# The softmax denominator's broadcast matmul in bf16 instead of f32, in a fused attention and MoE kernel

## The chip, the cores and the metric

The kernel runs on one Trainium2 chip as one program on all 8 cores. The metric is the device time of a run in microseconds, that of the slowest core. A core has TensorE (PE, matmuls into PSUM), VectorE (DVE), ScalarE (ACT, activation functions), GpSimd (POOL, which here only issues DMAs) and SyncE (SP, likewise).

## What is computed

The input x has 4 sequences of 4096 tokens with 1024 features. The layer is attention with 16 heads whose queries and keys are 6-vectors, followed by a mixture of 8 experts, each with a residual and a layer norm:

```python
x_bigram = concatenate([x, x_prev], -1)
L_q = exterior(x_bigram @ W1_q, x_bigram @ W2_q)   # per head, 6 values, normalized
L_k = exterior(x @ W1_k, x @ W2_k)
attn = einsum('bqhc,bkhc->bhqk', L_q, L_k @ _J6.T) * 6.0 ** (-0.5)
attn = softmax(where(causal, attn, -inf))
out = einsum('bhqk,bkhd->bqhd', attn, x @ W_v + b_v) @ W_o + b_o
x = layernorm(x + out)
# MoE: router softmax, top 2 of 8 experts, h = silu(x @ w_gate) * (x @ w_up), h @ w_down
x = layernorm(x + moe(x))
```

## The kernel before

Each core takes one sequence's keys and values (two cores share a sequence) and half of its query tiles: 16 tiles of 128 rows. The program has three blocks, one behind the other.

- The first block transposes x, projects values, keys and queries, and leaves `Vs` (values of 32 key tiles, per head 64 columns and a 65th of ones), `JLKT` (keys) and `LQT` (queries) in SBUF.
- The second block is attention with the output projection, the first layer norm and the router. It is the one that the change touches.
- The third block is the MoE, expert by expert, with weights loaded from HBM, and the last layer norm.

In the second block the query tiles are taken in four groups of four (`g`, 512 query columns at once). Group g needs K = 8g + 8 key chunks of 128. Heads are taken in eight pairs (a, b). For each key chunk `kc` (a step):

1. `emit_score` (L444): PE computes the scores of a and of b (L457, keys by queries, 128 by up to 512 into one of three PSUM banks `pS`), and ACT takes exp(scale * score) into `PT`, bf16 (L467). For the last 8 chunks DVE multiplies 128 columns by the causal mask (L474).
2. `emit_av` (L480): PE accumulates `Vs[kc, h]` (65 columns) by `PT` into `pAV0` or `pAV1`, 65 partitions by 512 (L488). The 65th row, from the column of ones, is the sum of the exponentials, that is the softmax denominator. There is one bank for even heads and one for odd heads, so the next pair's first accumulation waits until the last pair's has been read.

The division is a chain for each head, in three functions. `emit_chain_pre` (L504): DVE copies row 64 of `pAV` to `srow` on one partition (L509), then PE spreads it over 64 partitions by a matmul of a row of 64 ones with `srow` (L519) into `pWO[0:64, 512:1024]`. `emit_chain_act` (L523): ACT takes Ln of it (L525) and Exp of minus that (L528), which gives 1/sum in `rbr`. `emit_chain_post` (L533): DVE multiplies `pAV[0:64]` with `rbr` into `attnT`, bf16 (L536), and so frees the bank.

The order is written out by hand in the loop over pairs (L547). Within step kc the scores of kc are issued ahead of the AV matmuls of kc - 1. The last pair's chains are put into the next pair's first steps: `pre` and `act` of head a and then of head b behind the scores of step 0, `post` of both behind the scores of step 1. On PE the two L519 of a border so stand between the scores of step 0 and those of step 1, and on ACT the Ln and Exp of both heads stand between the exponentials of step 0 and step 1. All chains use the same `srow` and the same PSUM columns: the copy of b waits for the matmul of a (semaphore `rbm`), and the matmul of b waits for the Exp of a (semaphore `rbr`). Behind the last pair of a group the chains run alone: that of head 14 twice (L570, L571), then that of head 15. Then follow, for each of the four tiles, the output projection (L585), the residual, the layer norm and the router.

Of the kernel before, what the change touches and what calls it, by code (L numbers as in the profile page):

```python
# [8 lines left out]
F32 = mybir.dt.float32  # L9
BF16 = mybir.dt.bfloat16  # L10
# [59 lines left out]
def build_program(debug=0, phases=3):  # L70
# [45 lines left out]
    with ExitStack() as _st0:  # L116
# [11 lines left out]
        with ExitStack() as _st1:  # L128
# [4 lines left out]
            with ExitStack() as _stA:  # L133
# [30 lines left out]
                P = Prog()  # L164
# [184 lines left out]
                if debug >= 3:  # L349
                    JL_D3 = P.val("jl")  # L350
                    P.emit("gpsimd", lambda g: g.dma_start(out=dbg["kk"], in_=kk_sb[:]),
                           waits=[("jl", JL_D3)], inc="dbgs", inc_n=16)
# [4 lines left out]
                if debug >= 1:  # L357
                    JL_D = P.val("jl")
                    P.emit("gpsimd", lambda g: g.dma_start(out=dbg["vs"], in_=Vs[:]),
                           waits=[("jl", JL_D)], inc="dbgs", inc_n=16)  # L360
# [9 lines left out]
                       waits=[("wA", W_SETUP), ("dbgs", P.val("dbgs"))])  # L370
# [8 lines left out]
            with ExitStack() as _stB:  # L379
                sbB = lambda *a: _stB.enter_context(nc.sbuf_tensor(*a))  # L380
# [7 lines left out]
                
                wo_sb = sbB("wo_sb", [128, 8, 1024], BF16)
                bob = sbB("bob", [128, D], F32)  # L390
                srow_t = sbB("srow", [1, 512], F32)
                ones1 = sbB("ones1", [1, 64], F32)
                
                rbl_t = sbB("rbl", [64, 512], F32)
                rbr0 = sbB("rbr0", [64, 512], F32)
# [27 lines left out]
                P = Prog(cnt1)  # L423
                PT = [PT0, PT1, PT2, PT3]
                pS, pAV = [pS0, pS1, pS2], [pAV0, pAV1]
                pWO = pWO0
# [4 lines left out]
                    out=wo_sb[:], in_=wo_h.rearrange("(dc p) n -> p dc n", p=128)), inc="wB", inc_n=16)  # L431
                P.emit("gpsimd", lambda g: g.dma_start(out=bob[:], in_=bob_h), inc="wB", inc_n=16)
                W_B = P.val("wB")
                P.emit("vector", lambda v: v.memset(ones1[:], 1.0), waits=[("bar1", 5)])
                P.emit("vector", lambda v: v.drain(), inc="xt")
                ONES_RDY = P.val("xt")

# [56 lines left out]
                for g in range(NG):  # L494
# [4 lines left out]
                        waits=[("bar1", 5), ("msk", P.cnt.get("_mskuse_%d" % (g - 1), 0))],  # L499
# [4 lines left out]
                    def emit_chain_pre(hh):  # L504
                        hbb = hh % 2
                        srw = [("av", av_counts[hh])]
                        if rbm_vals:
                            srw.append(("rbm", max(rbm_vals.values())))
                        P.emit("vector", lambda v, hbb=hbb: v.tensor_copy(  # L509
                            srow_t[0:1, :], pAV[hbb][64:65, :]), waits=srw)  # L510
                        P.emit("vector", lambda v: v.drain(), inc="sr")  # L511
                        sr_vals[hh] = P.val("sr")
                        rw = [("sr", sr_vals[hh]), ("xt", ONES_RDY)]
                        prev_rbr = rbr_vals[hh - 1] if (hh - 1) in rbr_vals else last_rbr
                        if prev_rbr:
                            rw.append(("rbr", prev_rbr))
                        rw.append(("y1a", P.val("y1a")))
                        def rbmm(te):
                            return te.matmul(pWO[0:64, 512:1024], ones1[:], srow_t[0:1, :], start=True, stop=True)  # L519
                        P.emit("tensor", rbmm, waits=rw, inc="rbm")  # L520
                        rbm_vals[hh] = P.val("rbm")

# [19 lines left out]
                    def emit_chain(hh):  # L542
                        emit_chain_pre(hh)
                        emit_chain_act(hh)
                        emit_chain_post(hh)

                    for p in range(8):  # L547
                        a, b = 2 * p, 2 * p + 1
                        prev_a = prev_b = None
                        for kc in range(K):  # L550
                            sinfo_a = emit_score(g, a, kc)
                            sinfo_b = emit_score(g, b, kc)
                            if p >= 1:
                                if kc == 0:
                                    emit_chain_pre(2 * p - 2)
                                    emit_chain_act(2 * p - 2)
                                    emit_chain_pre(2 * p - 1)
                                    emit_chain_act(2 * p - 1)
                                elif kc == 1:
                                    emit_chain_post(2 * p - 2)  # L560
                                    emit_chain_post(2 * p - 1)
                            if kc >= 1:
                                emit_av(g, a, kc - 1, prev_a)
                                emit_av(g, b, kc - 1, prev_b)
                            prev_a, prev_b = sinfo_a, sinfo_b
                        emit_av(g, a, K - 1, prev_a)
                        emit_av(g, b, K - 1, prev_b)
                        av_counts[a] = P.val("av") - 1
                        av_counts[b] = P.val("av")
# [5 lines left out]
                    for qq in range(4):  # L575
# [4 lines left out]
                            waits=[("bar1", 5), ("y1a", P.val("y1a"))], inc="xqd", inc_n=16)  # L580
                        def womm(te, qq=qq):
                            ins = None
                            for cp in range(8):
# [11 lines left out]
                               waits=[("wo", WO_T), ("xqd", P.val("xqd"))])  # L595
# [14 lines left out]
                               waits=[("v1", P.val("v1"))])  # L610
# [4 lines left out]
                               waits=[("sd1", P.val("sd1"))])  # L615
# [6 lines left out]
                        def tph(te, qt=qt):  # L622
                            ins = None
                            for dc in range(8):
# [4 lines left out]
                               waits=[("tpf", P.val("tpf"))])  # L629
                        P.emit("vector", lambda v: v.drain(), inc="xft")  # L630
                        def tpl(te):
                            ins = None
                            for dc in range(8):
# [4 lines left out]
                               waits=[("tpf", P.val("tpf"))])  # L638
# [5 lines left out]
                        def rtmm(te, qb=qb):  # L644
# [3 lines left out]
                            for src, w in srcs:  # L648
# [8 lines left out]
                            waits=[("rt", P.val("rt"))])  # L657
# [3 lines left out]
                            waits=[("rmax", P.val("rmax"))])  # L661
# [3 lines left out]
                               waits=[("rexp", P.val("rexp"))])  # L665
# [27 lines left out]
                if debug >= 2:  # L693
                    P.emit("gpsimd", lambda g: g.dma_start(out=dbg["acc"], in_=acc_t[:]),
                           waits=[("xf", P.val("xf"))], inc="dbgs", inc_n=16)
                    P.emit("gpsimd", lambda g: g.dma_start(out=dbg["comb"], in_=comb_t[:]),
                           waits=[("cmb", P.val("cmb"))], inc="dbgs", inc_n=16)
                    P.emit("gpsimd", lambda g: g.dma_start(out=dbg["attnT"], in_=attnT[:]),
                           waits=[("ate", P.val("ate"))], inc="dbgs", inc_n=16)
# [6 lines left out]
                       waits=[("wB", W_B), ("dbgs", P.val("dbgs"))])  # L706
# [8 lines left out]
        with ExitStack() as _stD:  # L715
# [23 lines left out]
            P = Prog(cnt2)  # L739
# [5 lines left out]
            for t in range(NSLOT):  # L745
                def tpx(te, t=t):
                    ins = None
                    for dc in range(8):
# [4 lines left out]
                       waits=[("bar2", 5), ("tpf", P.val("tpf"))])  # L753
# [3 lines left out]
            for e in range(NE):  # L757
                P.emit("gpsimd", lambda g, e=e: g.dma_start(  # L758
                    out=wg_sb[:], in_=wg_h[e].rearrange("(dc p) (hc q) -> p hc dc q", p=128, q=128)),
                    waits=[("bar2", 5), ("gmm", 44 * e)], inc="wg", inc_n=16)  # L760
                P.emit("gpsimd", lambda g, e=e: g.dma_start(
                    out=wu_sb[:], in_=wu_h[e].rearrange("(dc p) (hc q) -> p hc dc q", p=128, q=128)),
                    waits=[("bar2", 5), ("umm", 44 * e)], inc="wu", inc_n=16)
                P.emit("gpsimd", lambda g, e=e: g.dma_start(
                    out=wd_sb[:], in_=wd_h[e].rearrange("(hc p) n -> p hc n", p=128)),
                    waits=[("bar2", 5), ("dmm", 16 * e)], inc="wd", inc_n=16)

            for e in range(NE):
                for tc in range(4):
                    for hc in range(NHC):  # L770
                        gi = (tc * NHC + hc) % 2
                        def gmm(te, hc=hc, tc=tc, gi=gi, e=e):
                            ins = None
                            for dc in range(8):
# [5 lines left out]
                               waits=[("wg", 16 * (e + 1)), ("xft", XFT_ALL),  # L780
                                      ("sg", P.val("sg") - 1)], inc="gmm")
                        def umm(te, hc=hc, tc=tc, gi=gi, e=e):
                            ins = None
                            for dc in range(8):
# [5 lines left out]
                               waits=[("wu", 16 * (e + 1)), ("hm", P.val("hm") - 1)], inc="umm")  # L790
                        P.emit("scalar", lambda s, gi=gi: s.activation(sG[gi][:], pG[gi][:], AF.Silu),  # L791
                               waits=[("gmm", P.val("gmm")), ("hm", P.val("hm") - 1)])
# [3 lines left out]
                            waits=[("sg", P.val("sg")), ("umm", P.val("umm"))])  # L796
                        P.emit("vector", lambda v: v.drain(), inc="hm")
                HM_E = P.val("hm")
                for t in range(NSLOT):
                    def dmm(te, t=t):  # L800
                        ins = None
                        for hc in range(NHC):
# [7 lines left out]
                           waits=[("wd", 16 * (e + 1)), ("hm", HM_E), ("acc", P.val("acc"))],  # L810
                           inc="dmm")
                    if e == NE - 1:
# [3 lines left out]
                            waits=[("dmm", P.val("dmm"))])  # L816
                    else:
# [3 lines left out]
                            waits=[("dmm", P.val("dmm"))])  # L821
                    P.emit("vector", lambda v: v.drain(), inc="acc")  # L822
                    if e == NE - 1:
                        ob = t % 2
                        P.emit("vector", lambda v: v.tensor_scalar(st2[:, 0:1], st2[:, 0:1], 1.0 / D, None, ALU.mult),
                               waits=[("acc", P.val("acc"))])
# [8 lines left out]
                               waits=[("ln2", P.val("ln2"))])  # L835
# [5 lines left out]
                            waits=[("sd2", P.val("sd2")), ("out", 16 * t)])  # L841
# [3 lines left out]
                            waits=[("eo", P.val("eo"))], inc="out", inc_n=16)  # L845
# [71 lines left out]
```

How the kernel before makes its waits and increments, by code:

```python
    def replay(self, eng_name, handle, sems):  # L51
        for fn, waits, inc, inc_n in self.ops[eng_name]:
            for s, v in waits:
                handle.wait_ge(sems[s], v)
            ins = fn(handle)
            if inc is not None:
                if ins is None:
                    raise RuntimeError(f"op with inc {inc} returned no instruction")
                ins.then_inc(sems[inc], inc_n)
```

## Time and profile before

| what | value |
|---|---|
| times of two runs | 4463.73 and 4864.91 us |
| their median | 4664.32 us |
| the profiled execution, its own time | 4461.65 us |
| its span on the slowest core (core 4) | 4458.6 us |
| spans of the 8 cores | 4441.5 to 4458.6 us |
| mean granted TensorE clock of the 8 cores | 0.768 to 0.770 |
| busy: PE, weight loads, DVE, ACT, POOL | 3320.7, 1306.4, 1192.7, 952.0, 95.1 us |

The span goes from a core's first instruction to its last; the time of a run is 3 us more in the profiled execution. Busy times are sums over the whole span and say nothing on which engine a stage waits for. The granted clock is the share of the full 2.4 GHz that TensorE gets; 0.50 is the lower of its two levels, 1.2 GHz. The profile also has groups of instructions by line, the sums of who waited for whom, and the instructions in order of time, in which a bracket behind an instruction gives how long its engine was idle before it and what ended that. In a name such as `pS` the number of the buffer is left out.

### The profile page before, as it was taken

How to read it: one execution, taken by the hardware profiler on the slowest of the kernel's cores; microseconds unless marked ns; L12 is line 12 of the kernel's file. 1: busy time of each engine (PE TensorE's matmuls, PEld its weight loads, DVE VectorE, ACT ScalarE, POOL GpSimd, SP SyncE). 2: the span in 40 equal slices, each digit the busy share in tenths (PEclk: the TensorE clock that was granted, in tenths of full speed). 3: DMA queues.
4: the chain of work that ended last, by engine and by line, in shares of the span. 5: the costliest groups of instructions: out<-in, count | busy, mean ns of one | idle time of the engine just before them, and what ended most of it. 6: DMA issues, size and time to landing. Idle time of an engine off the chain costs nothing. (4 is left out here: it accounts for less than half of the span.)

```text
span 4458.5 us, 49278 instructions; the slowest of 8 cores (4441.5 to 4458.6 us)
## 1 busy us (share of the span) xinstructions
PE 3320.7 (74%) x14263; PEld 1306.4 (29%) x14476; DVE 1192.7 (27%) x3454; ACT 952.0 (21%) x1948; POOL 95.1 (2%) x42
## 2 busy tenths in 40 slices
PE   3444432556866896799945979898898979899896
PEld 1222222112112111111113434343343434344342
DVE  3444454233123113211142121121212112121126
ACT  0000000323533563466610101010010101011010
POOL 0000000000000000000000000000000000000000
PEclk8777655555555555555556999999999999999999
DMA  3111122000000000000007060515114051513301
GB/s 69 34 34 34 42 77 62 17 8 15 1 8 14 1 1 12 10 1 1 1 15 78 1 65 14 52 27 52 27 19 60 1 52 27 52 27 30 49 1 76
DMA packets 215020, 129.85 MB, mean 29 GB/s; under 512 B 188640, under 2 KB 188640, under 8 KB 214768
## 3 DMA queue, kind: packets, MB, share of 16 engines
q0 software_dynamic: 200944, 76.35, 14.7%
q1 hardware_dynamic: 13824, 50.34, 3.5%
q8 instruction: 134, 2.20, 0.2%
q14 instruction: 118, 0.97, 0.1%
HBM read 192.51 MB, written 8.39 MB: 45 GB/s over the span
## 5 line engine op out<-in xcount | busy, mean ns | idle before, releaser
L804 PE MATMUL pD<-wd_sb,ht 128*128 128x512 bf16 x2760 | 624.7, 379 | 200.6 <-DVEq L822 189.4
L488 PE MATMUL pAV<-PT,Vs 128*65 128x512 bf16 (+3 forms) x1280 | 624.4, 563 | 105.3 <-DVEq L539 55.0
L467 ACT ACTIVATE PT<-pS 128x512 bf16<-128x512 f32 (+3 forms) x1280 | 613.0, 531 | 384.7 <-PE pS L457 372.6
L785 PE MATMUL pU<-xfT,wu_sb 128*128 128x512 bf16 x2760 | 661.7, 380 | 25.6 <-DMA wu_sb<-w_up 22.6
L775 PE MATMUL pG<-xfT,wg_sb 128*128 128x512 bf16 x2759 | 661.9, 380 | 4.3 <-DVEq L754 1.4
L791 ACT ACTIVATE sG<-pG 128x512 bf16<-128x512 f32 x352 | 210.1, 597 | 1748.1 <-PE pG L775 1748.1
L794 DVE TENSOR_TENSOR ht<-sG,pU 128x512 bf16<-128x512 bf16 x352 | 241.8, 687 | 997.5 <-PE pU L785 997.5
L804 PEld LDWEIGHTS pD<-wd_sb,ht 128*128 128x128 bf16 x2816 | 266.2, 97 | 559.1 <-issue 256.5
L785 PEld LDWEIGHTS pU<-xfT,wu_sb 128*128 128x128 bf16 x2816 | 275.8, 98 | 356.5 <-issue 25.2
L775 PEld LDWEIGHTS pG<-xfT,wg_sb 128*128 128x128 bf16 x2816 | 276.0, 98 | 335.0 <-issue 4.3
L457 PE MATMUL pS<-LQT,JLKT 6*128 6x512 bf16 (+3 forms) x1280 | 358.0, 537 | 4.4 <-ACT PT L467 2.2
L474 DVE TENSOR_TENSOR PT<-PT,masks_g 128x128 bf16<-128x128 bf16 x512 | 115.4, 225 | 831.9 <-ACT PT L467 777.1
L818 DVE SCALAR_TENSOR_TENSOR acc<-pD,comb,acc 128x1024 bf16<-128x1024 f32 x112 | 143.7, 1283 | 582.1 <-PE pD L804 582.1
L488 PEld LDWEIGHTS pAV<-PT,Vs 128*65 128x65 bf16 x1280 | 140.4, 140 | 402.0 <-issue 395.8
L287 PE MATMUL pTk<-ident,Lsc 128*6 128x128 bf16 x768 | 28.7, 301 | 304.2 <-DVEq L279 304.2
L519 PE MATMUL pWO<-srow,ones 1*64 1x512 f32 x136 | 131.5, 1068 | 108.7 <-DVEq L511 61.6
L457 PEld LDWEIGHTS pS<-LQT,JLKT 6*128 6x128 bf16 x1280 | 71.6, 99 | 430.8 <-issue 425.2
L302 PE MATMUL pV<-wvks,xT 128*128 128x512 bf16 (+1 forms) x740 | 183.3, 416 | 3.9 <-issue 3.1
L214 PE MATMUL pT<-ident,xab 128*128 128x128 bf16 x512 | 64.7, 306 | 127.2 <-DVEq L210 127.2
L258 ACT ACTIVATE rln<-ssb 128x16 f32<-128x16 f32 x48 | 10.3, 215 | 689.0 <-DVEq L257 689.0
L625 PE MATMUL pT<-ident,acc 128*128 128x128 bf16 x128 | 16.2, 306 | 145.1 <-DVEq L620 145.1
L302 PEld LDWEIGHTS pV<-wvks,xT 128*128 128x128 bf16 x768 | 84.6, 124 | 96.2 <-issue 69.1
(113 smaller groups left out, 1339.2 us busy)
## 6 DMA issues: line engine op xcount, KB each, us to landing
wg_sb<-w_gate POOLq DMA_DIRECT2D x8, 2816.0 KB, 25.2
wu_sb<-w_up POOLq DMA_DIRECT2D x8, 2816.0 KB, 24.3
wd_sb<-w_down POOLq DMA_DIRECT2D x8, 2816.0 KB, 18.9
xa<-x_kv SPq DMA_DIRECT2D x32, 512.0 KB, 3.6
xa<-xq SPq DMA_DIRECT2D x16, 512.0 KB, 3.6
xa<-xq_prev SPq DMA_DIRECT2D x16, 512.0 KB, 3.6
xqr<-xq SPq DMA_DIRECT2D x16, 512.0 KB, 3.5
out_q<-outst SPq DMA_DIRECT2D x16, 512.0 KB, 2.6
```

Of the source, the lines that this page charges most:

```text
L302: ins = te.matmul(pV[b][:, n0:n1], xT[b][:, dc, :], wvks[:, dc, n0:n1], start=(dc == 0), stop=(dc == 7))
L457: return te.matmul(pS[sb][:, off:512], JLKT[32 * gr:32 * gr + 6, m, kc * 128:(kc + 1) * 128], LQT[32 * gr:32 * gr + 6, m, g * 512 + off:(g ...
L467: P.emit("scalar", lambda s, sb=sb, off=off, pslot=pslot, ncols=ncols: s.activation(PT[pslot][:, 0:ncols], pS[sb][:, off:512], AF.Exp, bia ...
L474: P.emit("vector", lambda v, pslot=pslot, jj=jj, ii=ii, g=g: v.tensor_mul(PT[pslot][:, 0:128], PT[pslot][:, 0:128], masks_g[:, jj, ii, :]) ...
L488: return te.matmul(pAV[hb][:, off:512], Vs[:, kc, h, :], PT[pslot][:, 0:ncols], start=(kc == 0), stop=(kc == K - 1))
L519: return te.matmul(pWO[0:64, 512:1024], ones1[:], srow_t[0:1, :], start=True, stop=True)
L775: ins = te.matmul(pG[gi][:], wg_sb[:, hc * 8 + dc, :], xfT[:, dc, tc * 512:(tc + 1) * 512], start=(dc == 0), stop=(dc == 7))
L785: ins = te.matmul(pU[gi][:], wu_sb[:, hc * 8 + dc, :], xfT[:, dc, tc * 512:(tc + 1) * 512], start=(dc == 0), stop=(dc == 7))
L791: P.emit("scalar", lambda s, gi=gi: s.activation(sG[gi][:], pG[gi][:], AF.Silu), waits=[("gmm", P.val("gmm")), ("hm", P.val("hm") - 1)])
L794: P.emit("vector", lambda v, gi=gi, hc=hc, tc=tc: v.tensor_tensor(ht_sb[:, hc, tc * 512:(tc + 1) * 512], sG[gi][:], pU[gi][:], ALU.mult), ...
L804: ins = te.matmul(pD[:, nb * 512:(nb + 1) * 512], ht_sb[:, hc, t * 128:(t + 1) * 128], wd_sb[:, hc, nb * 512:(nb + 1) * 512], start=(hc == ...
L818: P.emit("vector", lambda v, e=e, t=t: v.scalar_tensor_tensor(acc_t[:, t, :], pD[:], comb_t[:, t, e:e + 1], acc_t[:, t, :], ALU.mult, ALU. ...
```

## The change

The row of sums is written as bf16 instead of f32, and the ones are bf16, so the matmul that spreads the row takes two bf16 operands. Its result in PSUM stays f32. The instructions of the program, their order on every engine and all waits are the same; the copy in L509 becomes a copy with a cast.

```diff
-                srow_t = sbB("srow", [1, 512], F32)
-                ones1 = sbB("ones1", [1, 64], F32)
+                srow_b = sbB("srow_b", [1, 512], BF16)
+                ones1b = sbB("ones1b", [1, 64], BF16)
...
-                P.emit("vector", lambda v: v.memset(ones1[:], 1.0), waits=[("bar1", 5)])
+                P.emit("vector", lambda v: v.memset(ones1b[:], 1.0), waits=[("bar1", 5)])
...
                         P.emit("vector", lambda v, hbb=hbb: v.tensor_copy(
-                            srow_t[0:1, :], pAV[hbb][64:65, :]), waits=srw)
+                            srow_b[0:1, :], pAV[hbb][64:65, :]), waits=srw)
...
                         def rbmm(te):
-                            return te.matmul(pWO[0:64, 512:1024], ones1[:], srow_t[0:1, :], start=True, stop=True)
+                            return te.matmul(pWO[0:64, 512:1024], ones1b[:], srow_b[0:1, :], start=True, stop=True)
```

## Rows read from the trace of the kernel before

**Rows 1.** the page, busy tenths of PE and its granted clock in 40 slices
```profile
PE   3444432556866896799945979898898979899896
...
PEclk8777655555555555555556999999999999999999
```

**Rows 2.** stretches of core 4: us, busy us per engine, granted clock, DMA share, GB/s
```profile
1800.00:2330.00 530.00, 440.51 (x1285) 104.02 (x1288) 95.82 (x269) 281.15 (x558) 0.00 (x0) 0.52 0.01 5
...
2400.00:4458.00 2058.00, 1834.23 (x8272) 816.77 (x8440) 453.02 (x576) 218.81 (x384) 73.69 (x21) 1.00 0.29 36
```

**Rows 3.** groups by line and form: count, busy us, mean ns, idle before
```profile
L457 PE MATMUL pS<-LQT,JLKT 6*128 6x512 bf16 x896 | 276.4, 602 | 4.2 <-ACT PT L467 2.0 <-PEq L62 1.3 <-ACTq L662 0.9
...
L519 PE MATMUL pWO<-srow,ones 1*64 1x512 f32 x136 | 131.4, 1068 | 108.7 <-DVEq L511 61.6 <-ACTq L530 45.8 <-issue 1.4
...
L509 DVE COPY srow<-pAV 1x512 f32<-1x512 f32 x68 | 46.5, 684 | 81.3 <-PE pWO L519 71.0 <-PE pAV L488 6.5 <-issue 3.8
L536 DVE TENSOR_TENSOR attnT<-pAV,rbr 64x512 bf16<-64x512 f32 x68 | 46.5, 683 | 127.7 <-ACTq L530 125.0 <-issue 2.6
```

**Rows 4.** who waited for whom, 800 to 2330 us: total us, times, longest us
```profile
ACT rbl L525 <- PE pWO L519: 167.0, 68, 4.3
...
DVE srow L509 <- PE pWO L519: 71.0, 28, 2.9
```

**Rows 5.** order of time, a border in group 3: start us, us, operation
```profile
1864.68 0.69 DVE L509 COPY srow<-pAV 1x512 f32<-1x512 f32 x1 [0.19 <-PE pAV L488]
...
1864.89 0.64 PE L457 MATMUL pS<-LQT,JLKT 6*128 6x512 bf16 x2
1865.64 1.08 ACT L467 ACTIVATE PT<-pS 128x512 bf16<-128x512 f32 x2 [1.86 <-PE pS L457]
...
1865.86 1.93 PE L519 MATMUL pWO<-srow,ones 1*64 1x512 f32 x2 [0.33 <-issue]
1867.89 0.59 ACT L525 ACTIVATE rbl<-pWO 64x512 f32<-64x512 f32 x1 [1.16 <-PE pWO L519]
...
1869.45 1.93 PE L519 MATMUL pWO<-srow,ones 1*64 1x512 f32 x2 [1.66 <-ACTq L530]
...
1871.48 0.59 ACT L525 ACTIVATE rbl<-pWO 64x512 f32<-64x512 f32 x1 [2.30 <-PE pWO L519]
...
1872.98 1.08 ACT L467 ACTIVATE PT<-pS 128x512 bf16<-128x512 f32 x2 [0.21 <-issue]
...
1873.83 0.60 PE L488 MATMUL pAV<-PT,Vs 128*65 128x512 bf16 x1 [1.33 <-DVEq L539]
```

**Rows 6.** order of time, a border in group 0
```profile
804.52 1.94 PE L519 MATMUL pWO<-srow,ones 1*64 1x512 f32 x2 [2.78 <-DVEq L511]
806.55 0.59 ACT L525 ACTIVATE rbl<-pWO 64x512 f32<-64x512 f32 x1 [3.58 <-PE pWO L519]
...
808.01 1.93 PE L519 MATMUL pWO<-srow,ones 1*64 1x512 f32 x2 [1.55 <-ACTq L530]
...
810.04 0.59 ACT L525 ACTIVATE rbl<-pWO 64x512 f32<-64x512 f32 x1 [2.19 <-PE pWO L519]
```

**Rows 7.** order of time, the end of group 3
```profile
2255.89 1.94 PE L519 MATMUL pWO<-srow,ones 1*64 1x512 f32 x2 [3.70 <-DVEq L511]
2257.93 0.59 ACT L525 ACTIVATE rbl<-pWO 64x512 f32<-64x512 f32 x1 [4.34 <-PE pWO L519]
...
2261.53 1.94 PE L519 MATMUL pWO<-srow,ones 1*64 1x512 f32 x2 [3.70 <-DVEq L511]
```

**Rows 8.** order of time, steps inside a pair of group 3
```profile
1838.14 0.61 PE L457 MATMUL pS<-LQT,JLKT 6*128 6x512 bf16 x2
...
1838.90 1.08 ACT L467 ACTIVATE PT<-pS 128x512 bf16<-128x512 f32 x2 [0.45 <-PE pS L457]
...
1839.68 0.61 PE L457 MATMUL pS<-LQT,JLKT 6*128 6x512 bf16 x2
```

**Rows 9.** stretches, as in rows 2, one of 20 us in group 3
```profile
1880.00:1900.00 20.00, 20.00 (x54) 3.79 (x52) 0.00 (x0) 14.17 (x27) 0.00 (x0) 0.50 0.00 1
```

## The prediction

> **What bounds the kernel now.** I read the slices of the page first, for the stages. In the last 18 slices (the MoE) the granted clock is at 9 tenths or more and PE is busy for 7 to 9 tenths in nearly all of them; in the slices before, from the fifth on, the clock is at 5 or 6 [rows 1]. The stretches say it in sums: in the attention stage, which ends at about 2330 us, PE stands at 0.52 of its clock (the 1.2 GHz level, with a little of the other), and the MoE stage holds 1834.23 us of PE work in 2058 us at 1.00 (2.4 GHz) [rows 2]. The change touches attention only, so the question is which wait ends last there. Inside a pair of heads PE is saturated: one step of the chunk loop takes 1839.68 - 1838.14 = 1.54 us, ACT needs 1.08 us of that for its two exponentials and then waits 0.45 us for PE [rows 8]. At the border between two pairs it is the other way round. The sums of who waits for whom show ACT waiting 167.0 us, in 68 waits, for the matmul of L519, and DVE's row copy waiting 71.0 us for it in 28 [rows 4]. PE in turn restarts only when the DVE multiply that ends the chain is done (the wait of 1.33 us at 1873.83) [rows 5]. 68 is the number of times that L519 is issued: (16 + 1) in each of 4 groups, since head 14's chain is issued twice.
>
> **What the profile shows of L519.** It has 136 records of 1068 ns for 68 issues, two per matmul, both of f32 with 512 columns; a bf16 matmul of 512 columns (L457, contraction over 6 rows) has one record, 602 ns [rows 3]. What counts is the time from its start to the start of what waits for it. For L519 that is 806.55 - 804.52 = 2.03 us and 810.04 - 808.01 = 2.03 us in group 0, 1867.89 - 1865.86 = 2.03 us in group 3, and 2257.93 - 2255.89 = 2.04 us at a group's end [rows 5 to 7]. For the bf16 matmul of L457 at the same clock it is 1865.64 - 1864.89 = 0.75 us [rows 5]. So each L519 on the path is worth 2.03 - 0.75 = 1.28 us. At 1.2 GHz 512 columns take 0.427 us, and 1.28 us is three times that: it looks as if f32 passed through the array four times (two in each record) and bf16 once.
>
> **The change part by part.**
> 1. The row of sums is written as bf16 (L509, 68 times). The nearest row that reads f32 from PSUM and writes bf16 with 512 columns is L536: 683 ns, against 684 for the copy now [rows 3]. Two edges: 0.68 us if the write type is free, as those rows say, and perhaps 0.34 us if the narrower type doubled the speed, which no row of a PSUM f32 source shows. I take nothing; of the fast end 40 copies would be on the path (28 first ones, 12 at the ends), 40 x 0.34 = 14 us, and on the other side I allow the same 0.1 us by which one hand-over differs from another, 4 us.
> 2. The ones are bf16 (one memset, before the stage): nothing.
> 3. L519 becomes a bf16 matmul of 1 row by 64 columns by 512. No row has this form; L457 is nearest. Its time from start to hand-over can hardly be under 0.6 us, its own length, nor over 2.03 us.
>
> Borders of group 0, seven of them. Both matmuls stand in one serial chain: copy, matmul A, Ln and Exp of A, matmul B (it writes the same PSUM columns, so it waits for A's Exp), Ln and Exp of B, then the exponentials of step 1 [rows 6]. ACT has finished its exponentials of step 0 long before matmul A ends. Each saves 1.28 us: 7 x 2.56 = 17.9 us.
>
> Borders of groups 1 to 3, 21 of them [rows 5]. Matmul A starts at 1865.86 as before, since it waits for the copy (1864.68 + 0.69). Its result would be there at 1866.61, but ACT is still at its two exponentials of step 0 until 1865.64 + 1.08 = 1866.72. So Ln of A starts at 1866.72 instead of 1867.89 and saves 1.17, not 1.28. Matmul B follows Ln of A by 1869.45 - 1867.89 = 1.56 us, at 1868.28, and Ln of B 0.75 us later, at 1869.03 instead of 1871.48: 2.45 us gained. The second copy could be late next. It starts when matmul A is done, 1866.61, takes 0.69, and the hand-over from a copy to L519 takes 1865.86 - 1865.37 = 0.49: ready at 1867.79, ahead of the 1868.28 by 0.49 us. PE's scores of step 1 stand behind matmul B and are done by about 1869.5, 1.0 us before ACT reaches them (at 1869.03 + 1.50, as 1872.98 - 1871.48 now). What restarts PE is the DVE multiply of head B, which hangs on the Exp of B, and this moves with it. Sum: 21 x 2.45 = 51.5 us.
>
> Group ends, four with three chains each [rows 7]. Nothing runs beside them (period 5.64 us): 12 x 1.28 = 15.4 us.
>
> Sum: 17.9 + 51.5 + 15.4 = 84.8 us. Nothing else moves on any engine: the program has the same instructions in the same order, no wait is added, no DMA. What follows (the output projection, the router, the weight loads of the MoE stage, which wait for the stage's barrier) starts earlier by what came before and stays as long. So the profiled execution's 4461.65 us becomes 4461.65 - 84.8 = 4376.9, say 4377 us, 1.90% less. The two runs shown are 4463.73 and 4864.91; the profiled one stands at the lower, and the median of the two, 4664.32, is no time that either had. I forecast against 4462 to 4464. The line at 2%, about what a measurement of this kernel can tell from no change, is at 89 us, 4 us beyond the sum.
>
> **Rivals.**
> - A. Only the second matmul of each border counts, because ACT's own exponentials or the copy hide the first. For it: in groups 1 to 3 ACT is busy behind the first. Against it: those exponentials end 1.17 us before Ln of A starts now [rows 5]. Time: (28 + 12) x 1.28 = 51.2 us, 4410 us.
> - B. The granted clock rises in attention, since PE's breaks at the borders get shorter. Then a step falls from 1.54 us to ACT's 1.08. Groups 1 to 3 have 8 x (8 + 16 + 24) = 384 steps of full width: 384 x 0.46 = 177 us more, 4200 us. Against it: in the stretch 1880 to 1900 PE is busy 20.00 of 20 us with no L519 in it, and the clock is 0.50 all through [rows 9]. Shorter breaks can't make PE denser than that. The Trainium skill speaks for this rival: "TensorE: Matmul & The Clock Gate", the section on the HAM clock gate, says that sustained matmul activity releases the throttle. In this trace it doesn't, with matmuls of 6 rows or 65 columns back to back.
> - C. The passes aren't what costs; a matmul of one row with its own weights hands over late for another reason, and the bf16 one is as slow. Time: 4462 us. Against it are the two records per matmul and the 0.75 us of L457 [rows 3, 5].
> - D. Slower: the MoE stage loses its clock. It is the only place with enough work: 2058 us at 1.00 [rows 2]. One of the two runs took 4864.91 - 4463.73 = 401 us more; if a lower granted clock in that stage is what such a run has, and if the changed kernel met it in its usual runs, the time would be 4377 + 401 = 4778 us. It decides from 85/401 = 21% of that loss on. For it is only that the eight cores might reach the stage closer together; against it, each core's attention shortens by the same amount, and the profiled execution holds 1.00. The Trainium skill states such a limit ("TensorE: Matmul & The Clock Gate", the HAM clock gate section: 13/16 of the clock once three cores of a die run dense matmuls). This trace disagrees with it as a standing rule: eight cores, 1.00.
>
> **How the numbers follow.** Forecast 0.76, A 0.09, B 0.05, C 0.06, D 0.04. The forecast's own range: the cast's 14 us to the fast side and 4 us to the other, the hand-over of ACT in groups 1 to 3 up to 0.2 us later or 0.1 earlier (21 times: 4 and 2 us), and the spread of executions (I allow 0.2%, 9 us): 4358 to 4394. To take in a part of A, the range is 4356 to 4400. Faster by over 2% (under about 4373 us): the forecast's lower part, 0.33 of all, and B: 0.38. Slower by over 2%: D, 0.04. Within 2%: the rest, 0.58.
>
> **What would show it.** L519 with 68 records of about 0.61 us; 0.75 us from its start to Ln; the 167.0 us that ACT waits for it down to 167.0 - 84.8 = 82 us; the border in group 3 (first copy to PE's restart, 1873.83 - 1864.68 = 9.15 us) at 6.7 us; group ends with a period of 4.36; attention over at about 2245 instead of 2330; steps inside a pair still at 1.54 us and clock 0.50; the MoE stage as long as before. The prediction is wrong if L519 hands over later than 0.85 us, if the cast of L509 isn't near 0.68 us, if the border shrinks by only one matmul, or if anything outside the borders changes by over 10 us.

## The result and the profile after

Over all runs shown with the result the median went from 4546.28 us (10 runs) to 4451.13 us (11 runs). Part of the runs of either kernel (5 of 10 before, 6 of 11 after) took longer, with a lower TensorE clock on one or both dies wherever the clocks are on record, so the ratio here and the times given with the experiments are those of the others, 4463.73 to 4487.62 us before and 4370.62 to 4374.99 us after. The ratio is 0.9785, with a 95% interval of 0.9761 to 0.9809: 2.15% less, and the interval has the line at 2% inside it. One of the five times before, 4487.62 us, stands apart from the rest (4463.73 to 4464.67); without it the ratio of the means would be 0.9795. The profiled execution took 4374.07 us (before: 4461.65), with spans of 4354.7 to 4372.4 us over the cores and a mean granted clock of 0.774 to 0.776.

The groups by line and form show what became of the matmul, the row copy and the Ln behind it (as in [rows 3]: count, busy us, mean ns, idle before):

```profile
L509 DVE CAST srow_b<-pAV 1x512 bf16<-1x512 f32 x68 | 46.6, 685 | 43.8 <-PE pWO L519 33.4 <-PE pAV L488 6.5 <-issue 3.8
...
L519 PE MATMUL pWO<-srow_b,ones1b 1*64 1x512 bf16 x68 | 40.8, 600 | 109.0 <-DVEq L511 61.4 <-ACTq L530 46.3 <-issue 1.3
L525 ACT ACTIVATE rbl<-pWO 64x512 f32<-64x512 f32 x68 | 40.2, 591 | 78.6 <-PE pWO L519 78.6
```

L519 has 68 records of 600 ns where it had 136 of 1068, and the cast takes 685 ns where the copy took 684. The waits, against [rows 4]:

```profile
ACT rbl L525 <- PE pWO L519: 78.6, 48, 3.0
...
PE pAV L488 <- DVEq L539: 55.0, 35, 3.6
...
DVE srow_b L509 <- PE pWO L519: 33.4, 28, 1.6
```

ACT's wait fell from 167.0 to 78.6 us, and from 68 waits to 48: in 20 cases the profile shows no idle time before Ln any more. They are the first matmuls of 20 of the 21 borders in groups 1 to 3. What PE waits for the multiply that ends the chain (L539 is the drain behind L536) stands at 55.0 us as before: in [rows 5] that wait begins at 1873.83 - 1.33 = 1872.50, when the border's second L519 is done (at 1871.38) and the second Exp runs, and it was never a part of what the matmul cost.

The same border of group 3 as in [rows 5], on core 4, in order of time:

```profile
1796.43 0.69 DVE L509 CAST srow_b<-pAV 1x512 bf16<-1x512 f32 x1 [0.19 <-PE pAV L488]
...
1797.39 1.09 ACT L467 ACTIVATE PT<-pS 128x512 bf16<-128x512 f32 x2 [1.86 <-PE pS L457]
...
1797.61 0.60 PE L519 MATMUL pWO<-srow_b,ones1b 1*64 1x512 bf16 x1 [0.36 <-issue]
1798.32 0.68 DVE L509 CAST srow_b<-pAV 1x512 bf16<-1x512 f32 x1 [1.20 <-PE pWO L519]
1798.36 0.58 ACT L525 ACTIVATE rbl<-pWO 64x512 f32<-64x512 f32 x1
...
1799.92 0.60 PE L519 MATMUL pWO<-srow_b,ones1b 1*64 1x512 bf16 x1 [1.72 <-ACTq L530]
...
1800.62 0.59 ACT L525 ACTIVATE rbl<-pWO 64x512 f32<-64x512 f32 x1 [0.97 <-PE pWO L519]
...
1802.12 1.08 ACT L467 ACTIVATE PT<-pS 128x512 bf16<-128x512 f32 x2 [0.21 <-issue]
...
1802.96 0.60 PE L488 MATMUL pAV<-PT,Vs 128*65 128x512 bf16 x1 [1.33 <-DVEq L539]
```

From the first copy to PE's restart it takes 1802.96 - 1796.43 = 6.53 us, where it took 9.15: 2.62 us less. Ln of the first head runs right behind the exponentials (no bracket, so no idle time before it), 0.75 us after the matmul's start; the second matmul hands over in 1800.62 - 1799.92 = 0.70 us. This border is the first of its group, and that is an exception. A later one of the same group:

```profile
2005.91 1.08 ACT L467 ACTIVATE PT<-pS 128x512 bf16<-128x512 f32 x2 [1.86 <-PE pS L457]
2006.19 0.60 PE L519 MATMUL pWO<-srow_b,ones1b 1*64 1x512 bf16 x1 [0.43 <-DVEq L511]
2006.89 0.59 ACT L525 ACTIVATE rbl<-pWO 64x512 f32<-64x512 f32 x1
```

Here the first matmul hands over in 0.70 us too, although the exponentials end at 2006.99 in their row. So it is at 17 of the 21 borders of groups 1 to 3, on every core; the three first borders of the groups have 0.75 or 0.76 us, and one has 0.98. At the end of group 3, on core 4:

```profile
2167.66 0.60 PE L519 MATMUL pWO<-srow_b,ones1b 1*64 1x512 bf16 x1 [3.70 <-DVEq L511]
2168.36 0.59 ACT L525 ACTIVATE rbl<-pWO 64x512 f32<-64x512 f32 x1 [3.01 <-PE pWO L519]
...
2171.96 0.60 PE L519 MATMUL pWO<-srow_b,ones1b 1*64 1x512 bf16 x1 [3.70 <-DVEq L511]
```

The period of a chain is 4.30 us instead of 5.64 [rows 7], 1.34 less. Outside of this nothing moved. A stretch of 20 us inside a pair, and the MoE stage (columns as in [rows 2] and [rows 9]):

```profile
1820.00:1840.00 20.00, 20.00 (x54) 3.87 (x52) 0.45 (x2) 14.18 (x27) 0.00 (x0) 0.50 0.00 1
```

```profile
2400.00:4370.00 1970.00, 1766.84 (x8092) 782.17 (x8090) 437.57 (x554) 206.45 (x363) 73.66 (x21) 1.00 0.30 35
```

PE is saturated at the lower clock as before, and the MoE stage has its 2.4 GHz.

For small differences I use one measure of the profiled executions, the attention interval: from the first matmul of L519 (or what stands in its place) to the first weight load of the MoE stage, as a mean over the 8 cores. In the kernel before it is 1577.3 us (1576.3 to 1579.1), in the changed one 1487.8 us (1487.4 to 1488.6): 89.5 us less. What lies behind it, the MoE stage, is 2073.9 us against 2075.5 as a mean, but 2069.0 to 2079.9 from core to core, so the run time of one execution can hide or feign 5 us. The interval differs by 1 to 4 us from core to core, and its mean is the steadier measure.

### The profile page after: what moved, and what is told of

The parts are those of the page before. It is cut to its first block and busy times, and to the rows that moved or that the text cites. A ratio compares the mean times of both kernels' runs of the same rounds, so it can differ in the third digit from the quotient of the medians.

```text
span 4372.4 us, 49355 instructions; the slowest of 8 cores (4354.7 to 4372.4 us)
## 1 busy us (share of the span) xinstructions
PE 3248.8 (74%) x14408; PEld 1296.1 (30%) x14408; DVE 1193.0 (27%) x3454; ACT 950.8 (22%) x1948; POOL 95.1 (2%) x42
## 5 line engine op out<-in xcount | busy, mean ns | idle before, releaser
L457 PE MATMUL pS<-LQT,JLKT 6*128 6x512 bf16 (+3 forms) x1280 | 357.9, 537 | 4.5 <-ACT PT L467 2.2
L457 PEld LDWEIGHTS pS<-LQT,JLKT 6*128 6x128 bf16 x1280 | 71.7, 99 | 397.9 <-issue 392.3
L519 PE MATMUL pWO<-srow_b,ones1b 1*64 1x512 bf16 x68 | 40.8, 600 | 109.0 <-DVEq L511 61.4
## 6 DMA issues: line engine op xcount, KB each, us to landing
wg_sb<-w_gate POOLq DMA_DIRECT2D x8, 2816.0 KB, 30.4
```

What stands on the lines that cost most here:

```text
L457: return te.matmul(pS[sb][:, off:512], JLKT[32 * gr:32 * gr + 6, m, kc * 128:(kc + 1) * 128], LQT[32 * gr:32 * gr + 6, m, g * 512 + off:(g ...
```

## The experiments

All are built on the changed kernel. The interval meant is the attention interval.

**e1_four_times.** The bf16 matmul is issued four times.

```diff
                         def rbmm(te):
-                            return te.matmul(pWO[0:64, 512:1024], ones1b[:], srow_b[0:1, :], start=True, stop=True)
+                            ins = None
+                            for _ in range(4):
+                                ins = te.matmul(pWO[0:64, 512:1024], ones1b[:], srow_b[0:1, :], start=True, stop=True)
+                            return ins
```

> The changed kernel with the bf16 matmul of L519 issued four times into the same place. Theory (each L519 is a serial hand-over and costs the array time of its passes, 0.43 us per 512 columns at 1.2 GHz, whatever the type): 0.70 + 3 x 0.43 = 1.98 us from the first of four to Ln, against 2.03 for f32, so nearly all of the gain is given back: about 4372 + 68 x 1.28 = 4459 us, within 5 us of the kernel before. Rival C (the f32 type itself, its weight load or the f32 row is what costs): hand-over well under 2 us and a time near 4372.

Measured: 4462.61 and 4463.11 us, interval 1573.0 us. In order of time, a border of group 3:

```profile
1865.82 1.88 PE L521 MATMUL pWO<-srow_b,ones1b 1*64 1x512 bf16 x4 [1.66 <-ACTq L533]
...
1867.80 0.59 ACT L528 ACTIVATE rbl<-pWO 64x512 f32<-64x512 f32 x1 [2.25 <-PE pWO L521]
```

1867.80 - 1865.82 = 1.98 us, as forecast, against 2.03 in f32. 85.2 of the 89.5 us are given back with the type still bf16. So the gain is array time: three bf16 matmuls more, of (1.98 - 0.70) / 3 = 0.43 us each, take nearly all of it back. Rival C, against which the hand-over of 0.70 us in the result already stood, is out. The f32 matmul has 0.05 us more each, 68 x 0.05 = 3.4 us, which the interval shows as 4.3. That an f32 matmul is four passes is inferred from this nearly equal length and from its two records; no run shows the passes themselves.

**e2_first_only.** bf16 for one matmul in two at the borders. `srow_b` lies in a tile that is free at that time.

```diff
+                        sr_, on_ = (srow_b, ones1b) if (hh % 2 == 0 and hh < 14) else (srow_t, ones1)
...
-                            srow_b[0:1, :], pAV[hbb][64:65, :]), waits=srw)
+                            sr_[0:1, :], pAV[hbb][64:65, :]), waits=srw)
...
-                            return te.matmul(pWO[0:64, 512:1024], ones1b[:], srow_b[0:1, :], start=True, stop=True)
+                            return te.matmul(pWO[0:64, 512:1024], on_[:], sr_[0:1, :], start=True, stop=True)
```

> bf16 only for the first of the two matmuls at the 28 borders; the second one and all chains at the group ends are f32 as before. Theory (serial chain, nothing hides the first): group 0 saves 7 x 1.34, groups 1 to 3 save 21 x 1.28, 36 us in all, about 4428 us. Rival A (only the second counts, the first is hidden behind ACT's exponentials): no gain, 4464 us.

Measured: 4427.72 to 4430.96 us (four runs), interval 1541.4 us, 35.9 less than before where 36 was forecast. A border of group 3 shows both kinds beside each other:

```profile
1841.37 0.60 PE L523 MATMUL pWO<-xlo,ones1b 1*64 1x512 bf16 x1 [0.33 <-issue]
...
1842.13 0.58 ACT L529 ACTIVATE rbl<-pWO 64x512 f32<-64x512 f32 x1
...
1843.69 1.93 PE L523 MATMUL pWO<-srow,ones 1*64 1x512 f32 x2 [1.72 <-ACTq L534]
...
1845.72 0.59 ACT L529 ACTIVATE rbl<-pWO 64x512 f32<-64x512 f32 x1 [2.30 <-PE pWO L523]
```

The first one counts, so rival A is out. This border is again the first of its group, where Ln comes 0.76 us after the matmul's start; at 17 of the 21 borders of groups 1 to 3 it comes after 0.69 or 0.70 us, as in group 0, so the exponentials of ACT hide almost nothing of the first matmul.

**e4_once14.** One chain of each group's end is left out; head 14's chain was issued twice, with the same result both times.

```diff
-                    emit_chain(14)
                     emit_chain(14)
                     emit_chain(15)
```

> The changed kernel with head 14's chain issued once instead of twice at each group's end. Theory: a chain that runs alone has a period of 5.64 - 1.34 = 4.30 us, four of them go: 17 us, about 4355 us. Rival: if the DVE and ACT parts overlapped with the projection, under 5 us.

Measured: 4359.53, 4359.87, 4360.45, 4377.53 and 4382.25 us; interval 1471.2 us, 16.6 less than the changed kernel. The four chains were serial to the full, 4.15 us each by the interval and 4.30 by the period. The run time shows only some 12 us of it in the three lowest runs, within the spread of the MoE stage. The profiled execution is the one of 4382.25 us, and it shows why it is longer. The same stretch of the MoE stage on core 6 and on core 4 (columns as in [rows 2]):

```profile
3080.00:3230.00 150.00, 149.02 (x569) 62.42 (x578) 24.76 (x36) 21.71 (x37) 0.00 (x0) 0.82 0.05 9
3080.00:3230.00 150.00, 148.92 (x691) 67.36 (x689) 29.54 (x43) 25.42 (x43) 4.69 (x1) 1.00 0.09 17
```

With PE busy all through on both, core 6 got 0.82 of the clock and through 569 matmuls, core 4 1.00 and through 691. Core 7 has 0.82 there like core 6. The interval, which ends before, doesn't see it.

**e5_two_halves.** On e4, each head of a pair gets its own row buffer and its own half of the PSUM tile, with the waits kept per half.

```diff
-                            srow_b[0:1, :], pAV[hbb][64:65, :]), waits=srw)
+                            srow2[hbb][0:1, :], pAV[hbb][64:65, :]), waits=srw)
...
-                        prev_rbr = rbr_vals[hh - 1] if (hh - 1) in rbr_vals else last_rbr
+                        prev_rbr = half_rbr[hbb]
...
-                            return te.matmul(pWO[0:64, 512:1024], ones1b[:], srow_b[0:1, :], start=True, stop=True)
+                            return te.matmul(pWO[0:64, hbb * 512:(hbb + 1) * 512], ones1b[:], srow2[hbb][0:1, :], start=True, stop=True)
```

> As e4_once14, and heads a and b have a row buffer and a half of the PSUM tile each, so the second matmul no longer waits for the first head's Exp. Theory (serial chain with ACT next in line): Ln of b starts 0.2 us after Exp of a ends, 0.65 us earlier at the borders of group 0 and 0.76 in the others: 7 x 0.65 + 21 x 0.76 = 21 us, about 4334 us. Rival (PE or DVE is already the bound at the borders after the change): within 5 us of e4_once14.

Measured: 4336.99 and 4337.21 us; interval 1449.4 us, 21.8 less than e4 (forecast 21). A border of group 3:

```profile
1816.60 0.68 DVE L510 CAST srow_a<-pAV 1x512 bf16<-1x512 f32 x1 [0.26 <-PE pAV L489]
...
1817.78 0.60 PE L520 MATMUL pWO<-srow_a,ones1b 1*64 1x512 bf16 x1 [0.40 <-DVEq L512]
...
1818.72 0.60 PE L520 MATMUL pWO<-srow_c,ones1b 1*64 1x512 bf16 x1 [0.34 <-issue]
...
1819.92 0.59 ACT L527 ACTIVATE rbl<-pWO 64x512 f32<-64x512 f32 x1 [0.15 <-issue]
...
1820.82 0.60 PE L489 MATMUL pAV<-PT,Vs 128*65 128x512 bf16 x1 [0.95 <-DVEq L542]
...
1822.27 0.61 PE L489 MATMUL pAV<-PT,Vs 128*65 128x512 bf16 x1 [0.84 <-DVEq L542]
```

The second matmul no longer waits for the first head's Exp: it starts 0.94 us after the first one. Ln of the second head now follows at 1819.92, 1.20 us after its matmul's start, since ACT comes from the first head's Exp and waits for no matmul.

**e6_two_halves_f32.** e5 with f32 for row and ones.

```diff
-                srow2 = [sbB("srow_a", [1, 512], BF16), sbB("srow_c", [1, 512], BF16)]
+                srow_t = sbB("srow", [1, 512], F32)
...
+                srow2 = [srow_t, y1b_t]
```

> e5_two_halves with f32 row, ones and matmul (four passes). Theory: the two matmuls now follow each other on PE, so Ln of b is late by the second one's passes only: 3.90 us after the start of the first matmul against 2.20 in bf16, 1.70 x 28 = 48 us, and 8 chains at the group ends at 1.34 = 11 us: e5 (4337) + 58 = 4395 us. So the type is worth 58 us where the chain is less serial, not 86 (64 x 1.34). Rival (the second is hidden in whole): e5 + 40 x 1.34 or less, under 4390; rival (each matmul counts in full, wherever it stands): 4337 + 86 = 4423 us.

Measured: 4394.60 us (one run); interval 1505.3 us, 55.9 more than e5. In order of time:

```profile
1815.86 1.93 PE L521 MATMUL pWO<-srow,ones 1*64 1x512 f32 x2 [0.40 <-DVEq L513]
1817.59 1.91 PE L521 MATMUL pWO<-y1b,ones 1*64 1x512 f32 x2
1817.89 0.59 ACT L528 ACTIVATE rbl<-pWO 64x512 f32<-64x512 f32 x1 [1.23 <-PE pWO L521]
...
1819.60 0.59 ACT L528 ACTIVATE rbl<-pWO 64x512 f32<-64x512 f32 x1 [0.41 <-PE pWO L521]
```

The second f32 matmul runs under the first head's Ln and Exp, and ACT waits only 0.41 us for it. Ln of the second head comes 1819.60 - 1815.86 = 3.74 us after the first matmul's start, in e5 1819.92 - 1817.78 = 2.14: 1.60 us at each of 28 borders, where 1.70 were forecast. The type is worth 55.9 us here and not 64 x 1.34 = 86. So what the same edit brings depends on how serial the code around it is.

**e3_wide.** A row of 128 ones and 128 output partitions.

```diff
-                ones1b = sbB("ones1b", [1, 64], BF16)
+                ones1b = sbB("ones1b", [1, 128], BF16)
...
-                            return te.matmul(pWO[0:64, 512:1024], ones1b[:], srow_b[0:1, :], start=True, stop=True)
+                            return te.matmul(pWO[0:128, 512:1024], ones1b[:], srow_b[0:1, :], start=True, stop=True)
```

> The changed kernel with a row of 128 ones and 128 output partitions in L519 instead of 64. Theory: the hand-over of 0.70 us in place of L457's 0.75 comes from the width of the weights (64 columns less to run through at 1.2 GHz, 0.053 us), so it becomes 0.75 and the time 68 x 0.05 = 3.5 us longer, about 4376 us. Rival (it comes from one row instead of 6, or from L457 running as a pair): stays 0.70.

Measured: 4369.69 us (one run), interval 1485.2 us, 2.6 less than the changed kernel. My theory is refuted, even in its sign, and the hand-over is 0.68 us. This makes up 68 x 0.02 = 1.4 us of the 2.6; the rest stays open. The groups of L519:

```profile
L519 PE MATMUL pWO<-srow_b,ones1b 1*128 1x512 bf16 x68 | 39.4, 579 | 109.1 <-DVEq L511 61.4 <-ACTq L530 46.4 <-issue 1.3
L519 PEld LDWEIGHTS pWO<-srow_b,ones1b 1*128 1x128 bf16 x68 | 6.7, 99 | 140.4 <-issue 140.4
```

The wider matmul is 21 ns shorter, 579 against 600 ns, and its weight load 99 ns against 122 for 64 columns. The Trainium skill knows the second ("TensorE: Matmul & The Clock Gate", the section on weight-path perf modes): a fast weight load is used when there are 128 weights and the type isn't FP32. The trace agrees with the sign, 99 ns for 128 columns against 122 ns for 64. Why L457's hand-over is 0.05 us longer than L519's stays open.

**e7_bank_freed.** On e5: DVE copies all 65 rows of the accumulator to SBUF as bf16, and this frees the bank; the chain works from the copy and is spread over the next pair's steps.

```diff
-                            srow2[hbb][0:1, :], pAV[hbb][64:65, :]), waits=srw)
+                            av_sb[hbb][:], pAV[hbb][:]), waits=srw)
                         P.emit("vector", lambda v: v.drain(), inc="sr")
                         sr_vals[hh] = P.val("sr")
+                        avbank_free[hbb] = ("sr", P.val("sr"))
...
-                                    emit_chain_act(2 * p - 2)
                                     emit_chain_pre(2 * p - 1)
-                                    emit_chain_act(2 * p - 1)
                                 elif kc == 1:
-                                    emit_chain_post(2 * p - 2)
+                                    emit_chain_mm(2 * p - 2)
+                                    emit_chain_mm(2 * p - 1)
+                                    emit_chain_act(2 * p - 2)
+                                elif kc == 2:
+                                    emit_chain_exp(2 * p - 2)
+                                elif kc == 3:
+                                    emit_chain_act(2 * p - 1)
+                                    emit_chain_post(2 * p - 2)
+                                elif kc == 4:
+                                    emit_chain_exp(2 * p - 1)
+                                elif kc == 5:
                                     emit_chain_post(2 * p - 1)
```

> On e5_two_halves: DVE copies all 65 rows of an accumulator to SBUF as bf16 (one instruction as before), which frees the bank for the next pair at once; the matmul reads row 64 of the copy, and Ln, Exp and the final multiply are spread over steps 1 to 5 of the next pair. Theory (the chain's latency at the border is what is left to gain): PE restarts some 2.8 us after the first copy starts instead of 5.8, 21 x 3.0 = 62 us; group 0 about 20, the ends 12: about 4243 us. Rival (ACT, with 2.5 us of chain in steps that leave it 0.45 us each, becomes the bound): half of it, about 4290 us.

Measured: 4266.63 to 4267.93 us (three runs), 0.9557 of the kernel before (0.9516 to 0.9598); interval 1381.8 us, 67.6 less than e5. That is 4.4% less than the kernel before and some 105 us less than the changed one. But 94 us were forecast. A border of group 3:

```profile
1815.20 0.69 DVE L510 CAST av_sb<-pAV 65x512 bf16<-65x512 f32 x1 [0.26 <-PE pAV L489]
...
1816.49 0.69 DVE L510 CAST av_sb<-pAV 65x512 bf16<-65x512 f32 x1 [0.61 <-issue]
...
1818.33 1.06 PE L489 MATMUL pAV<-PT,Vs 128*65 128x512 bf16 x2
...
1821.40 1.06 PE L489 MATMUL pAV<-PT,Vs 128*65 128x512 bf16 x2
...
1823.13 1.06 PE L489 MATMUL pAV<-PT,Vs 128*65 128x512 bf16 x2
...
1823.62 1.08 ACT L468 ACTIVATE PT<-pS 128x512 bf16<-128x512 f32 x2 [0.18 <-issue]
...
1824.87 1.06 PE L489 MATMUL pAV<-PT,Vs 128*65 128x512 bf16 x2
...
1826.67 1.06 PE L489 MATMUL pAV<-PT,Vs 128*65 128x512 bf16 x2
```

PE restarts 3.13 us after the first copy instead of the 2.8 forecast. Three steps with an Ln or an Exp of the chain on ACT take 1823.13 - 1821.40 = 1.73 us, 1.74 and 1.80 instead of 1.53, and in them ACT no longer waits for PE: it is the bound, as the rival said.

The sum of 94 us hides two errors of opposite sign. I took the time of a group from its first score matmul to its last accumulation, as a mean over the cores. In groups 1 to 3 e7 is 30.4 us shorter than e5, not 62; in group 0 26.9, not 20; at the group ends (from there to the first matmul of the projection) 11.7, as forecast; together 69.0, where the interval has 67.6. So a border of groups 1 to 3 gained 1.4 us and not 3.0, about the half that the rival gives; for the whole the rival's 4290 us are 22 too many, since group 0 gained more. The 3.0 were 5.8 - 2.8, the restart of the second head in e5 against that of the first head in e7. Like against like, the second head restarts 1822.27 - 1816.60 = 5.67 us after the first copy in e5 and 3.56 in e7 (0.43 behind the 3.13), 2.1 us earlier, and the three longer steps take 0.7 of it back.

**e8_bank_freed_four.** e7 with the matmul issued four times, as in e1.

> e7_bank_freed with the bf16 matmul issued four times, that is the array time of f32. Theory (off the chain, but PE is saturated in the steps): the passes count as PE work, 2 x 3 x 0.43 = 2.57 us at each of 28 borders, 72 us, and some 10 us at the ends: about 82 us above e7. Rival (off the critical path the type is free): within 10 us of e7.

Measured: 4338.34 to 4339.98 us (three runs); interval 1454.0 us, 72.2 more than e7. Off the chain of waits the passes count nearly as much as on it. By the times of the groups, taken as in e7, groups 1 to 3 are 53.7 us longer, 2.56 at each of 21 borders, which is 2 x 3 x 0.43 in full. Group 0 is 14.2 us longer where 18 were forecast, and the ends 6.2 where 10 were: a part is hidden there. That the interval is at 28 x 2.57 = 72 is chance.

## Why the prediction was right or wrong

- **The time as a number was wrong.** The median of all runs is 4451.13 us, outside of 4356 to 4400. The step that failed is the one that says "I forecast against 4462 to 4464". It took the lower of two runs that lay 401 us apart as the kernel's time and gave a lower clock in the usual runs a chance of 0.04, as if only the change could bring it. The runs showed that either kernel has it in about half of its runs: the median before was 4546.28 us and not 4464, and the one after lies 74 us above the forecast. A forecast of a median has to take the spread of the kernel before along.
- **The mechanism was right.** Shown by e1 (85.2 of 89.5 us come back with four bf16 matmuls) and e2 (the first matmul of a border counts). Against the profiled execution, 4374.07 us is 2.9 below the 4377 forecast, and the other runs at the same clock lie at 4371 to 4375.
- **The hand-over of a bf16 matmul was mis-sized.** I took 0.75 us from L457. It is 0.70 us. Each matmul was worth 1.34, not 1.28: 7 x 2.68 + 12 x 1.34 = 34.8 us in place of 33.3.
- **Ln behind ACT's exponentials was mis-sized.** I let Ln wait for the end of the exponentials in their row, a saving of 1.17 us. In the border shown it starts 1797.39 + 1.09 - 1798.36 = 0.12 us before that end, and at 17 of the 21 borders it comes 0.70 us after the matmul's start, so that the exponentials hide nothing. From the first copy to PE's restart the 21 borders save 55.7 us on core 4, 2.65 each, in place of 51.5. With both terms the sum is 90.5 us, and the interval shows 89.5.
- **The cast costs nothing:** right, 685 against 684 ns. **The second copy isn't late:** right, the second matmul still waits for Exp (the bracket at 1799.92). **Nothing outside the borders moves:** right; stretches inside a pair and the MoE stage are as before.
- **ACT's wait for L519** was to fall to 82 us; it is 78.6. **The end of group 3:** 4.36 forecast, 4.30 measured.
- **The range.** Its slow end is the sum of the terms given, 4 + 4 + 9. The fast end isn't: 14 + 2 + 9 is 25 us, which gives 4352 and not 4358. It changes nothing here.
- **The chances.** 0.58 stood on within 2%, 0.38 on faster by over 2%. The ratio of 2.15% lies with the second by a hair and its interval with neither; 0.1 of it is the one time of 4487.62 us. The 4.7 us missing in the sum are what put it near the line.
- **Rival B** (a higher clock) didn't come: 0.50 with PE busy for 20.00 of 20 us. **Rival D** didn't come in the profiled execution: the MoE stage is at 1.00. A lower clock there does exist, 0.82 on e4's cores 6 and 7. But the kernel before has longer runs at a lower clock too, so the change is not what brings them. That they all lose their time in the MoE stage isn't shown, since none of them was profiled.

## What to carry to other kernels

A small matmul in f32 on a serial chain costs its passes over again each time: look up its hand-over (its start to its consumer's start), not its share of busy time, and multiply by how often the chain is walked. Then ask what makes the chain serial. Here a shared PSUM region (22 us) and, with the chain held at the border, the late release of the accumulator's bank (68 us for both, which e7 changes together) came together to as much again as the type's 90. Look at more than one border before taking its rows for all: the first of a group was the exception. Where a kernel's runs spread by several per cent, forecast the ratio of the runs at the full clock and the median apart.

## What the runs showed of the hardware that was not expected

- A 1-row f32 matmul of 512 columns takes 2.03 us to hand over at 1.2 GHz, four bf16 ones of the same shape 1.98 us, one 0.70 us.
- An ACT instruction behind two exponentials starts 0.06 to 0.12 us before their end in the profile at 20 of 21 borders, so an end in a row is no earliest start of the next.
- Weights of one row by 128 columns load in 99 ns, 64 columns in 122 ns, and the matmul behind the wider load is 21 ns shorter.
- PE was busy for a whole stretch of 20 us in attention at 0.50 of its clock; the MoE stage ran at 1.00 on all eight cores in the profiled execution. What sets the two apart no run isolates.
- In e4's profiled execution cores 6 and 7 had 0.82 of the clock for 150 us of the MoE stage. With PE busy all through, core 6 got through 569 matmuls in this time, and core 4 at 1.00 through 691.
